# Two gated attention and expert layers on one core: the first norms' statistics on other engines, value gates as columns of the value product, slot tables in 16-bit pairs

## The chip, the cores and the metric

The kernel runs on one core of one Trainium2 chip. The metric is device time in microseconds for one launch. The text speaks of five engines: TensorE (PE; PEld is its weight load), VectorE (DVE), ScalarE (ACT), GpSimd (POOL) and SyncE (SP, which here only issues DMAs). L1691 is line 1691 of the kernel.

## The reference

`x` holds 16 sequences of 128 tokens of 256 values: T = 2048 tokens. Four residual steps follow each other:

```python
x = x + tanh(g_xattn[0]) * layernorm(x) * scan(0.9, ctx * ctx)        # along the sequence
x = x + tanh(g_ffn[0])   * moe0(layernorm(x))    # 8 experts, top 2 by softmax, capacity 640, gelu(a) * g, F = 512
x = x + tanh(g_xattn[1]) * attention(layernorm(x), ctx, ctx)          # causal and padding mask, bias in q, k, v
x = x + tanh(g_ffn[1])   * moe1(layernorm(x))    # 8 experts, top 2 by logits, silu, F = 1024
```

The experts work on rows that their router has chosen. In moe0 a row beyond an expert's capacity is dropped, so the place of each row in its expert's list has to be known: it is the count of earlier rows with the same choice.

## The kernel before

Tokens lie in 16 tiles of 128 rows (one tile is a sequence), taken in four quads q of four tiles (NQ = 4, QB = 4). `xs` holds x, `cx` the context, each 128x4096 in fp32. Every engine has its own program, written out by hand; what orders them is semaphores, and on each engine the order of the calls. `link` makes VectorE wait for its own instruction.

**Prologue** (from the start to the first expert product at L1691). Per quad: VectorE takes the statistics of the norm of x (`norm_stats(0, q)`, L991 and L994: four BATCH_NORM_STATS2 and four aggregates), ScalarE makes rstd of them (`root`, L656 and L658), VectorE the product mean x rstd (`coefs`, L1002), ScalarE the normalised rows (`normalise`, L665). GpSimd squares the context quad (L497); TensorE multiplies it by the decay triangle (`retention`, L1556: two fp32 products of 512 columns, four records); VectorE multiplies rows and retained context (`retained`, L1038) and adds them to xs (`added`, L1044). TensorE turns the new rows (`rows`, L1516), ScalarE copies them out of PSUM (`rows_out`, L692), and TensorE makes the router's logits (`rows_router`, L1522, 16 records of 8 columns). The logits need no normalised rows: the gate matrix has its column means taken off it beforehand (`router_sums`, `sums_out`, L1063), and 1/std scales a row's logits only where probabilities are wanted. VectorE takes the two best (`choose`, L1009 and L1012). The statistics of the second norm, on the rows after the addition, are again bn_stats on VectorE (`norm_stats(1, q)`), and ScalarE writes the rows normalised by them (`normalise1`), which SP stores to `xn_rows[0]` in DRAM.

Between these, TensorE also makes products which only the attention stage uses: the turned context (`context`), its values (`values`, L1522, 16 records of 256 columns), the product Wq^T Wk with its bias terms (`weights`), and the value gates: Wv^T times the second router's matrix (`value_weights`), then context times that (`value_gates`, 16 records of 8 columns), which VectorE adds a bias to (L1138). `busy(n)` is n products of constants with no use for their result.

**Tables** (layer 0). `one_hots` (L1087 to L1092), a product with a triangle (`ranks`, L1659 to L1663), `pick` (L1102 to L1110): each row's place in its expert's list, split into the number of a 128-slot block and the slot in it. `maps` writes three one-hot arrays in 16-bit floats: `oha` (L1123; which of NA = 46 blocks, for the 32 groups of rows), `by_slot` (L1127; the same times the slot's number, from `slot_wide`), and `ohb` in four parts (L1131; which of 128 slots; 128x1024 each). `invert` (L1671, 32 products) turns them into a list of row numbers by slot. `turned_slots` (L1115, L1116) makes `row_x`, and GpSimd gathers the rows by indirect DMA, 128 a time (`gather0`, L519), once `xn_rows[0]` is complete. `gates0` (L1167 to L1179) makes the gates out of the probabilities. TensorE turns the gathered rows (`xt0`, L1703), ScalarE and VectorE split them into a high and a low part (L742, L1208), and the experts begin (`hid0`, `out0`, L1691). Each expert takes its weights from `raw`, split in the same way (`win0`, `wout0`; L733 and L1197, L738 and L1203).

**Transition and attention** (240 to 321 us). After expert 7: `context(2)`, `context(3)`, `value_gates(2)`, `value_gates(3)`, `values(2)`, `values(3)`, 16 fillers, and then per quad `rows_turned`, `queries`, `router(1, t)`, `scores`, `mixed`, `attended`. VectorE meanwhile adds the experts' results (`joined(0)`: L1265 and the statistics), then runs `value_gates(3)`, `values_joined(2)` (L1279), `coefs(2, 0)`. GpSimd does a part of the additions (`share`). Then the tables of layer 1 follow in the same form as in layer 0, and 20 pairs of row tiles through layer 1's experts.

The core of the VectorE order before:

```python
norm0(0); slot_wide copy; coefs(0, 0); retained(0); added(0)
norm0(1); coefs(0, 1); norm_stats(1, 0); norm0(2); retained(1); coefs(1, 0); added(1); coefs(0, 2)
wg minus its means; norm_stats(1, 1); norm0(3); retained(2); added(2); coefs(1, 1); coefs(0, 3)
cb copy; norm_stats(1, 2); retained(3); added(3); norm_stats(1, 3)
choose(0); coefs(1, 2); choose(1); coefs(1, 3); choose(2); choose(3); one_hots(0)
```

## Time and profile before

| | |
|---|---|
| median of 3 runs | 570.4 us (569.59 to 573.92) |
| the profiled execution | 573.94 us, of which its span is 572.0 us |
| granted TensorE clock, mean over the span | 0.967 of full speed |
| busy in the span: PE, PEld, DVE, ACT, POOL | 531.3, 492.7, 350.6, 321.8, 254.4 us |
| prologue, to the first expert product | 76.1 us |
| layer 0 experts | 76.1 to 239.7 us |
| transition and attention, tables of layer 1 | 239.7 to 332.5 us |
| layer 1 experts and output | 332.5 to 572.0 us |

The times of the trace count from the start of the span. "Busy" of PE counts a product of 8 columns like one of 512 as busy for its own time. PEclk is the share of full clock granted in a stretch: 1.00 is 2.4 GHz and 0.50 is 1.2 GHz. The chain of waits is followed back from the last instruction; what is in it sets the end, as the rest lies beside it.

### The profile page before, as it was taken

What the parts mean: (1) busy time and instruction counts of PE and PEld (TensorE: products, weight loads), DVE (VectorE), ACT (ScalarE), POOL (GpSimd) and SP (SyncE); (2) the same over time, 40 slices, a digit from 0 to 9 for tenths busy, and PEclk for the clock granted to TensorE, in tenths of its full rate; (3) what the DMA queues carried; (4) which work ended last, traced back from release to release, by engine and by line L of the source; (5) the groups of instructions that cost most, each with busy time, mean ns of one, the idle gap of its engine ahead of it and who ended that gap; (6) DMA issues with size and microseconds to landing.
All of it is one profiled execution on the core that took longest, in us unless ns stands there. A gap on an engine that the chain in (4) does not pass through costs nothing.

```text
span 572.0 us, 11981 instructions
## 1 busy us (share of the span) xinstructions
PE 531.3 (93%) x3775; PEld 492.7 (86%) x3776; DVE 350.6 (61%) x834; ACT 321.8 (56%) x670; POOL 254.4 (44%) x284
## 2 busy tenths in 40 slices
PE   2899889999999999998996989999999999999993
PEld 1789789999999999986775879999999999999993
DVE  2888845765655675466687865565736574654742
ACT  3573345665656675425577646565746574654742
POOL 2400366664355542314000263555566456654554
PEclk9997699999999999979999899999999999999997
DMA  7944253445345353362023343654563545262233
GB/s 251 383 173 149 74 159 100 159 151 171 92 151 170 113 170 110 120 202 94 1 92 130 85 136 98 176 136 110 110 128 74 165 110 121 45 184 55 39 50 48
DMA packets 52453, 72.74 MB, mean 127 GB/s; under 512 B 7200, under 2 KB 43936, under 8 KB 52416
## 3 DMA queue, kind: packets, MB, share of 16 engines
q1 hardware_dynamic: 40752, 50.34, 27.3%
q0 software_dynamic: 11664, 21.94, 17.6%
q8 instruction: 19, 0.31, 0.2%
q14 instruction: 18, 0.15, 0.1%
HBM read 51.54 MB, written 20.73 MB: 126 GB/s over the span
## 4 chain that ended last, share of the span: by engine, by line
PE 80%; DVE 9%; DMA 3%; ACT 3%; issue 2%; POOL 1%; DVEq 0%; SPq 0%; POOLq 0%; ACTq 0%
PE PA L1691 27%; PE PD L1691 9%; PE PC L1691 8%; PE PC L1905 6%; PE PD L1905 6%; PE PC L1907 3%; PE PD L1907 3%; PE PB L1522 3%; PE PC L1522 2%; PE PD L1522 2%; PE PB L1703 2%; DMA xg<-xn_rows,row_x 2%; PE PB L1880 2%; DVE stats L991 1%; DMA cx<-ctx 1%
## 5 line engine op out<-in xcount | busy, mean ns | idle before, releaser
L1691 PE MATMUL PA<-xhi,w_parts 128*128 128x256 f32 (+1 forms) x880 | 182.8, 289 | 4.2 <-issue 2.1
L1691 PEld LDWEIGHTS PA<-xhi,w_parts 128*128 128x128 f32 x880 | 144.9, 190 | 8.1 <-issue 4.5
L1691 PE MATMUL PA<-xlo,w_parts 128*128 128x256 f32 (+1 forms) x440 | 125.9, 286 | 0.0
L1251 DVE TENSOR_TENSOR hlo<-cT_all,hhi 128x512 fp32r<-128x512 f32 x78 | 54.1, 693 | 96.7 <-ACT hhi L938 96.6
L936 ACT ACTIVATE cT_all<-PA 128x512 f32<-128x512 f32 x78 | 46.7, 599 | 91.2 <-PE PA L1691 90.4
L610 POOL DMA_INDIRECT out<-ys,row_o x38 | 65.0, 1712 | 71.2 <-DVE ys L1462 56.7
L1691 PEld LDWEIGHTS PA<-xlo,w_parts 128*128 128x128 f32 x440 | 83.7, 190 | 0.0
L519 POOL DMA_INDIRECT xg<-xn_rows,row_x x45 | 46.2, 1028 | 66.9 <-DVEq L1117 39.9
L528 POOL DMA_INDIRECT y_rows<-ys,row_y x40 | 41.8, 1045 | 55.5 <-ACT ys L763 53.3
L1905 PE MATMUL PC<-w_parts,hhi 128*128 128x512 f32 x160 | 58.4, 399 | 0.0
L586 POOL DMA_INDIRECT xg<-xn_rows,row_x x44 | 47.7, 1085 | 23.6 <-POOL slot_gate L604 8.7
L1691 PE MATMUL PC<-xhi,w_parts 128*128 128x256 f32 (+1 forms) x256 | 55.1, 293 | 0.0
L1905 PE MATMUL PD<-w_parts,hhi 128*128 128x512 f32 x144 | 52.5, 399 | 0.0
L1691 PE MATMUL PD<-w_parts,hhi 128*128 128x256 f32 x280 | 51.7, 285 | 0.4 <-DVE w_parts L1203 0.4
L938 ACT ACTIVATE hhi<-cT_all 128x512 fp32r<-128x512 f32 x78 | 49.3, 632 | 2.5
L1251 DVE TENSOR_TENSOR w_parts<-raw,w_parts 128x512 fp32r<-128x512 f32 x64 | 40.6, 686 | 10.4 <-ACT w_parts L805 10.2
L1907 PE MATMUL PC<-w_parts,hlo 128*128 128x256 f32 x160 | 45.0, 281 | 0.0
L1691 PEld LDWEIGHTS PD<-w_parts,hhi 128*128 128x128 f32 x280 | 43.6, 191 | 0.6 <-issue 0.6
L1691 PEld LDWEIGHTS PC<-xhi,w_parts 128*128 128x128 f32 x256 | 43.0, 190 | 0.0
L1907 PE MATMUL PD<-w_parts,hlo 128*128 128x256 f32 x144 | 40.5, 282 | 0.0
L1691 PE MATMUL PD<-w_parts,hlo 128*128 128x256 f32 x140 | 39.6, 283 | 0.0
L1691 PE MATMUL PC<-xlo,w_parts 128*128 128x256 f32 (+1 forms) x128 | 37.5, 293 | 0.0
(267 smaller groups left out, 1069.2 us busy)
## 6 DMA issues: line engine op xcount, KB each, us to landing
raw<-w SPq DMA_DIRECT2D x16, 1024.0 KB, 5.4
raw<-L_ffn_W_in SPq DMA_DIRECT2D x8, 1024.0 KB, 5.3
raw<-L_ffn_W_out SPq DMA_DIRECT2D x8, 512.0 KB, 4.0
y_rows<-ys SPq DMA_DIRECT2D x8, 512.0 KB, 6.8
xn_rows<-xn SPq DMA_DIRECT2D x8, 512.0 KB, 3.6
xs<-x SPq DMA_DIRECT2D x4, 512.0 KB, 7.4
cx<-ctx SPq DMA_DIRECT2D x4, 512.0 KB, 7.9
ys<-y_rows SPq DMA_DIRECT2D x4, 512.0 KB, 4.6
```

Source lines behind the costliest of these rows:

```text
L519: pool.indirect_dma_start(xg[:, s, :], None, xn_rows[0].ap(), bass.IndirectOffsetOnAxis(ap=row_x[:, e % E * CT + t:e % E * CT + t + 1], ax ...
L528: pool.indirect_dma_start(y_rows.ap(), bass.IndirectOffsetOnAxis(ap=row_y[:, e * CT + t:e * CT + t + 1], axis=0), ys[:, s, :], None).then_ ...
L586: pool.indirect_dma_start(xg1[j % SLOTS1], None, xn_rows[1].ap(), bass.IndirectOffsetOnAxis(ap=row_x[:, j:j + 1], axis=0)).then_inc(g1_in[ ...
L610: pool.indirect_dma_start(out, bass.IndirectOffsetOnAxis(ap=row_o[:, j:j + 1], axis=0), ys[:, j % SLOTS1, :], None, compute_op=ALU.add).th ...
L936: act.activation(group1(h1, g), PA[:, g % 2, :], ACT.Silu).then_inc(silu_done, 1)
L938: act.activation(group1(hhi, g), group1(h1, g), ACT.Copy).then_inc(h1_hi, 1)
L1251: return dve.tensor_tensor(dst, src, hi.bitcast(F32), ALU.subtract)
L1522: mm = pe.matmul(dst, a, b, start=(k == 0), stop=(k == len(lhs) - 1))
L1691: mm = pe.matmul(dst, a[k], b[k], start=(first and k == 0 and a is lhs_hi and b is rhs_hi), stop=(last and k == n - 1 and a is lhs_lo))
L1703: mm = pe.transpose(bank0(pair)[:, t - tiles_of(pair)[0], k, :], xg[:, s, k * P:(k + 1) * P], ident)
L1905: pe.matmul(y1_at(par, t), hhi[:, a:a + P], w_parts[:, :, at], start=(g == 0 and n == 0), stop=False)
L1907: mm = pe.matmul(y1_at(par, t)[:, 0:D], hlo[:, a:a + P], whi[:, at], start=False, stop=(g == GROUPS - 1 and n == 1))
```

## The change

It does seven things.

1. The second norm's mean comes from the router's product: the first gate matrix gets a ninth column of -1/256, so `lg[..., 8]` is minus the mean. ScalarE takes the variance with four Square activations and their accumulator per quad (`squares1`), and the root (`root1`). The four `norm_stats(1, q)` and `coefs(1, q)` leave VectorE. The rows are normalised by GpSimd (quads 0, 1, 3; four tensor_scalar each, after a product of its own) and by VectorE (quad 2, behind `one_hots(0)`), and by ScalarE no more.
2. SP's queue is reordered: x0, gates, ctx0, tables, x1, ctx1, the two routers' matrices, x2, ctx2, x3, ctx3, and then the attention's weights and biases. `load(0, 0, True)` goes ahead of the stores of `xn_rows`.
3. VectorE squares context quad 0, GpSimd the other three. The copies of `cb` and of the number tables are GpSimd's; `slot_wide` is gone.
4. TensorE's `context(0)`, `values(0)`, `weights`, `value_weights` go behind the four routers, on both sides of `ranks(0)`; the separate `value_gates` products are gone.
5. The value gates are eight more columns of the value product (`wide_values`: 264 columns); ScalarE copies values and gates out in four instructions a quad.
6. `oha`, `by_slot`, `ohb` are laid out in pairs of groups, and all operands of the three comparisons and products are 16-bit floats; in both layers.
7. In the transition the order on VectorE is `wide_gates(2)`, `values_joined(2)`, `joined(0)`, `wide_gates(3)`, `coefs(2, 0)`; the last values go out by ScalarE and get their bias from GpSimd; layer 1's first weight parts are made between the last five outputs of expert 7; 32 fillers for 16.

```diff
+        rhs_a = xflat[:, 0:MAP_BLOCKS * NA * NG // 2].bitcast(F16)\
+            .rearrange("p (m a g) -> p m a g", m=PAIRS_OF_GROUPS, g=PART)
+        by_slot, oha = (rhs_a[:, :, n * NA:(n + 1) * NA, :] for n in range(MAP_BLOCKS))
...
                 if q == 0:
-                    sp.dma_start(cf[:, :], cf_d).then_inc(cf_in, 16)
+                    sp.dma_start(gts[:, 0:2], g_xattn.partition_broadcast(P)).then_inc(g_in, 16)
+                    sp.dma_start(gts[:, 2:4], g_ffn.partition_broadcast(P)).then_inc(g_in, 16)
                 sp.dma_start(cx[:, q * QB:(q + 1) * QB, :],
                              ctxt[q * QB:(q + 1) * QB].rearrange("b p d -> p b d")).then_inc(ctx_in[q], 16)
                 if q == 0:
-                    sp.dma_start(gts[:, 0:2], g_xattn.partition_broadcast(P)).then_inc(g_in, 16)
-                    sp.dma_start(gts[:, 2:4], g_ffn.partition_broadcast(P)).then_inc(g_in, 16)
...
+                    sp.dma_start(cf[:, :], cf_d).then_inc(cf_in, 16)
+                if q == 1:
                     for n, w in enumerate((wg0, wg1T)):
-                        sp.dma_start(wg[:, n, :, 0:E], w.rearrange("(c p) e -> p c e", p=P)).then_inc(small_in, 16)
+                        sp.dma_start(wg[:, n, :, 0:E], w.rearrange("(c p) e -> p c e", p=P)).then_inc(wg_in, 16)
+            for n, w in enumerate((wq, wk, wvT)):
+                sp.dma_start(wqkv[:, n, :, :] if n < 2 else wvx[:, :, 0:D],
+                         w.rearrange("(c p) d -> p c d", p=P)).then_inc(small_in, 16)
+            for n, b in enumerate((bq, bk, bvc)):
+                sp.dma_start(bqk[:, n, :], b).then_inc(small_in, 16)
+            sp.dma_start(bvb[:, :], bv.partition_broadcast(P)).then_inc(small_in, 16)
...
+            sp.wait_ge(ret_done, NQ)
+            load(0, 0, True)
             for q in range(NQ):
-                if q == NQ - 1:
-                    sp.wait_ge(ret_done, NQ)
-                    load(0, 0, True)
-                sp.wait_ge(xn_ready, XN[1, q])
+                if q == 2:
+                    sp.wait_ge(xn1_vector, 1)
+                else:
+                    sp.wait_ge(xn1_pool, min(q, 2) + 1)
...
+            pool.wait_ge(cf_in, 16)
+            pool.tensor_copy(number_table[:, :, :], c("iota").unsqueeze(2).broadcast_to([P, P, PART]))
+            pool.tensor_copy(slot16[:, :], c("slot")).then_inc(table_ready, 1)
+            for t in range(1, NQ):
                 pool.wait_ge(ctx_in[t], 16)
                 if t >= 2:
                     pool.wait_ge(ret_done, t - 1)
                 pool.tensor_tensor(cx2[:, t % 2], cx[:, t * QB:(t + 1) * QB, :], cx[:, t * QB:(t + 1) * QB, :],
                                    ALU.mult).then_inc(sq_ready, 1)
...
+            pool.tensor_copy(cb[:, :], cf[:, CF["before"][0]:CF["ones"][1]]).then_inc(cb_ready, 1)
+            pool.wait_ge(small_in, 16 * 7)
+            pool.tensor_tensor(bqbk[:, :], bqk[:, 0, :], bqk[:, 1, :], ALU.mult).then_inc(wide_ready, 1)
+            for k in range(DC):
+                pool.tensor_tensor(bv_wide[:, k, :], c("ones"), bqk[:, 2, k:k + 1].broadcast_to([P, P]),
+                                   ALU.mult).then_inc(wide_ready, 1)
+            for q in range(NQ):
+                m = place(1, q)
+                pool.wait_ge(sd_ready, ROOT[1, q])
+                pool.tensor_tensor(nmr[:, m, :], lg[:, q * QB:(q + 1) * QB, E], rstd[:, m, :], ALU.mult)\
+                    .then_inc(coef1_ready, 1)
+                if q != 2:
+                    pool.wait_ge(coef1_ready, q + 1)
+                    pool.wait_ge(xn_out0[q % 2], 16 * (q // 2))
+                    for b in range(QB):
+                        ins = pool.tensor_scalar(xn[:, q % 2, b, :], xs[:, q * QB + b, :], rstd[:, m, b:b + 1],
+                                                 nmr[:, m, b:b + 1], ALU.mult, ALU.add)
+                    ins.then_inc(xn1_pool, 1)
...
+            share(1)
+            for n in range(3 * QB, 4 * QB):
+                value_bias(n)
+            for q in range(2, NQ):
...
+            def squares1(q):
+                act.wait_ge(lg_used, q + 1)
+                for b in range(QB):
+                    ins = act.activation(junk1[:, b, :], xs[:, q * QB + b, :], ACT.Square,
+                                         bias=lg[:, q * QB + b, E:E + 1], accum_out=mv[:, place(1, q), b, 1:2])
+                ins.then_inc(square1_ready, 1)
+            def root1(q):
+                act.wait_ge(square1_ready, q + 1)
+                root(1, q, scale=1.0 / D)
...
             root(0, 0)
             normalise(0, 0, xn0[0])
-            context_out(0)
             root(0, 1)
             normalise(0, 1, xn0[1])
+            sums_out()
+            rows_out(0)
+            root(0, 2)
+            normalise(0, 2, xn0[0])
+            squares1(0)
+            root(0, 3)
+            rows_out(1)
+            normalise(0, 3, xn0[1])
+            root1(0)
+            rows_out(2)
+            squares1(1)
+            root1(1)
+            rows_out(3)
+            squares1(2)
+            root1(2)
+            squares1(3)
+            root1(3)
+            weights_out()
+            value_weights_out()
+            context_out(0)
             values_out(0)
...
+            context_out(1)
             act.wait_ge(e_arg, 1)
...
+            for t in range(CT):
+                evac0(1, E - 1, [t])
+                if t < PIECES:
+                    split1(win_in[1], 16, win_hi[1], piece_in, (t,))
+            context_out(2)
+            context_out(3)
...
+            def normalised1(q):
+                m = place(1, q)
+                dve.wait_ge(coef1_ready, q + 1)
+                dve.wait_ge(xn_out0[q % 2], 16 * (q // 2))
+                for b in range(QB):
+                    ins = dve.tensor_scalar(xn[:, q % 2, b, :], xs[:, q * QB + b, :], rstd[:, m, b:b + 1],
+                                            nmr[:, m, b:b + 1], ALU.mult, ALU.add)
+                ins.then_inc(xn1_vector, 1)
             norm0(0)
-            dve.wait_ge(cf_in, 16)
-            link(dve.tensor_copy(slot_wide[:, :, :], c("slot").unsqueeze(2).broadcast_to([P, NG, NA])))
+            dve.wait_ge(ctx_in[0], 16)
+            dve.tensor_tensor(cx2[:, 0], cx[:, 0:QB, :], cx[:, 0:QB, :], ALU.mult).then_inc(square0_ready, 1)
             coefs(0, 0)
+            norm0(1)
+            coefs(0, 1)
             dve.wait_ge(tanh_ready, 1)
             retained(0)
             added(0)
-            norm0(1)
-            coefs(0, 1)
-            norm_stats(1, 0)
-            norm0(2)
-            retained(1)
-            coefs(1, 0)
-            added(1)
-            coefs(0, 2)
             dve.wait_ge(evac_done, EV1["s", 0])
+            dve.memset(wg[:, 0, :, E:E + 1], -1.0 / D)
             link(dve.tensor_tensor(wg[:, :, :, 0:E], wg[:, :, :, 0:E],
                                    wg_mean[:, :, :].unsqueeze(2).broadcast_to([P, 2, DC, E]), ALU.add))
             dve.sem_inc(wg_ready, 1)
-            norm_stats(1, 1)
+            norm0(2)
+            retained(1)
+            coefs(0, 2)
+            added(1)
+            copied(0)
             norm0(3)
             retained(2)
+            coefs(0, 3)
             added(2)
-            coefs(1, 1)
-            coefs(0, 3)
-            link(dve.tensor_copy(cb[:, :], cf[:, CF["before"][0]:CF["ones"][1]]))
-            dve.sem_inc(cb_ready, 1)
-            norm_stats(1, 2)
+            chosen(0)
+            copied(1)
             retained(3)
             added(3)
-            norm_stats(1, 3)
-            choose(0)
-            coefs(1, 2)
-            choose(1)
-            coefs(1, 3)
-            choose(2)
-            choose(3)
+            chosen(1)
+            copied(2)
+            chosen(2)
+            copied(3)
+            chosen(3)
...
+            def maps(layer):
+                def over_pairs(x, m, n):
+                    return x[:, m.start * PART:m.stop * PART].rearrange("p (m g) -> p m g", g=PART).unsqueeze(2)\
+                        .broadcast_to([P, m.stop - m.start, n, PART])
+                every = slice(0, PAIRS_OF_GROUPS)
+                dve.tensor_tensor(oha, over_pairs(high16, every, NA), number_table[:, 0:NA, :].unsqueeze(1)
+                                  .broadcast_to([P, PAIRS_OF_GROUPS, NA, PART]), ALU.is_equal).then_inc(oha_ready, 1)
+                dve.tensor_tensor(by_slot, oha, over_pairs(slot16, every, NA), ALU.mult).then_inc(slot_ready, 1)
                 for n in range(MAP_PARTS):
+                    m = slice(n * PAIRS_OF_GROUPS // MAP_PARTS, (n + 1) * PAIRS_OF_GROUPS // MAP_PARTS)
+                    dve.tensor_tensor(ohb[:, m, :, :], over_pairs(low16, m, P), number_table[:, :, :].unsqueeze(1)
+                                      .broadcast_to([P, m.stop - m.start, P, PART]), ALU.is_equal)\
                         .then_inc(map_ready, 1)
...
             one_hots(0)
+            normalised1(2)
...
             masks()
             split1(0, win_hi[1], win_lo[1], piece_in)
-            value_gates(2)
+            wide_gates(2)
...
+            values_joined(2)
             joined(0)
-            value_gates(3)
-            values_joined(2)
+            wide_gates(3)
             coefs(2, 0)
             for t in range(NQ - 1):
                 joined(t + 1)
                 if t >= 2:
                     attended(t - 2)
                 coefs(2, t + 1)
-                if t == 0:
-                    values_joined(3)
...
+            def wide_values(q):
+                pe.wait_ge(evac_done, max(EV1["cT", q], EV1["v", 0]) if q == 1 else EV1["cT", q])
                 cT = context_at(q)
                 for b in range(QB):
-                    mm = product(values_at(q)[:, b // 2, (b % 2) * D:(b % 2 + 1) * D],
-                                 [cT[:, k, b * P:(b + 1) * P] for k in range(DC)],
-                                 [wqkv[:, 2, k, :] for k in range(DC)])
+                    mm = product(value_banks(q)[b // 2][:, b % 2, 0:D + E],
+                                 [cT[:, k, b * P:(b + 1) * P] for k in range(DC)], [wvx[:, k, :] for k in range(DC)])
                 mm.then_inc(evac_ready, 1)
...
+            busy(2, early_fill)
             retention(0)
-            context(0)
-            busy(4)
-            values(0)
+            router_sums()
             retention(1)
             rows(0)
-            router_sums()
-            weights(0)
             retention(2)
-            weights(1)
+            rows_router(0)
+            retention(3)
             rows(1)
-            retention(3)
-            rows_router(0)
-            busy(5, PA)
+            pe.wait_ge(ret_used, 3)
+            busy(4, early_fill)
+            rows_router(1)
             rows(2)
-            rows_router(1)
-            busy(11, PA)
+            busy(4, early_fill)
+            rows_router(2)
             rows(3)
-            rows_router(2)
+            busy(4, early_fill)
             rows_router(3)
-            value_weights()
-            busy(6, PB)
...
+            weights(0)
             pe.wait_ge(cb_ready, 1)
             ranks(0)
-            value_gates(0)
+            weights(1)
+            value_weights()
+            context(0)
+            wide_values(0)
+            invert(0)
             context(1)
-            busy(9)
-            invert(0)
-            value_gates(1)
-            values(1)
-            pe.wait_ge(evac_done, EV1["v", 1])
+            wide_values(1)
...
+            pe.wait_ge(evac_done, EV1["cT", 1])
+            xt0(0, 0, 0, 0, filler=1)
             xt0(0, 0, 0, 1, filler=1)
+            pe.wait_ge(evac_done, EV1["v", 1])
             pe.wait_ge(target0_ready, 1)
...
             context(3)
-            value_gates(2)
-            value_gates(3)
-            values(2)
-            values(3)
-            for n in range(16):
-                pe.matmul(PA[:, 0, 0:P], ident, decay, start=True, stop=True)
+            pe.wait_ge(y0_evac, 2 + E * CT)
+            wide_values(2)
+            wide_values(3)
+            pe.wait_ge(values2_ready, 1)
+            pe.wait_ge(vg_ready, 3)
+            for n in range(32):
+                pe.matmul(PC[:, 0, 0:P], ident, decay, start=True, stop=True)
```

## Rows read from the trace of the kernel before

**Rows 1.** The page's chain that ended last: shares of the span by engine

```profile
PE 80%; DVE 9%; DMA 3%; ACT 3%; issue 2%; POOL 1%; DVEq 0%; SPq 0%; POOLq 0%; ACTq 0%
```

**Rows 2.** Chain of waits, 8 to 77 us: start us, length us, what

```profile
1.77 6.49 DMA cx<-ctx
...
62.89 3.35 PE PA L1522 x16
...
66.25 5.56 PE PC L1522 x16
...
71.83 1.03 ACT vv L687
...
76.12 1.00 PE PA L1691 x5
```

**Rows 3.** Timeline of VectorE, 0 to 95 us: start us, length us, then what

```profile
4.26 1.40 DVE L991 BATCH_NORM_STATS2 stats<-xs 128x6 f32<-128x256 f32 x4 [4.15 <-DMA xs<-x]
...
14.27 1.28 DVE L1038 SCALAR_TENSOR_TENSOR xg<-xg,tg,PA 128x1024 f32<-128x1024 f32 x1 [3.00 <-PE PA L1556]
...
19.56 1.88 DVE L1002 SCALAR_TENSOR_TENSOR nmr<-mv,rstd 128x4 f32<-128x4 f32 x1 [0.66 <-ACT rstd L658]
...
50.40 0.19 DVE L1087 CAST eidx<-topi 128x32 f32<-128x32 uint32 x1
...
54.85 1.69 DVE L1123 TENSOR_TENSOR xg<-sm,cf 128x1472 f16<-128x1472 f32 x1
...
56.57 0.93 DVE L1127 TENSOR_TENSOR xg<-xg,slot_wide 128x1472 f16<-128x1472 f16 x1
...
57.42 4.62 DVE L1131 TENSOR_TENSOR ys<-smi,cf 128x1024 f16<-128x1024 int32 x4
...
68.03 0.29 DVE L1167 TENSOR_REDUCE rr<-lg 128x16 f32<-128x128 f32 x1 [0.24 <-DVE vg L1138]
...
70.50 0.26 DVE L1179 TENSOR_TENSOR gates<-sm,rr 128x16 f32<-128x16 f32 x2
```

**Rows 4.** Timeline of ScalarE, 0 to 95 us

```profile
11.37 2.07 ACT L665 ACTIVATE xg<-xs,nmr,rstd 128x256 f32<-128x256 f32 x4 [0.37 <-DVEq L1003]
...
58.44 1.99 ACT L733 ACTIVATE w_parts<-raw 128x1024 fp32r<-128x1024 f32 x2
```

**Rows 5.** Timeline of TensorE, 0 to 80 us

```profile
10.37 3.75 PE L1556 MATMUL PA<-raw,cf 128*128 128x512 f32 x4 [10.37 <-POOL raw L497]
...
29.67 1.11 PE L1522 MATMUL PD<-wqkv 128*128 128x256 f32 x4
...
30.62 1.04 PE L1516 MATMUL PB<-cf,xs 128*128 128x128 f32 x8
...
33.21 1.85 PE L1522 MATMUL PD<-wg,xT 128*128 128x8 f32 x16
```

**Rows 6.** Timeline of GpSimd, 0 to 95 us

```profile
19.52 1.89 POOL L497 TENSOR_TENSOR raw<-cx 128x1024 f32<-128x1024 f32 x1 [0.80 <-DMA cx<-ctx]
...
64.27 1.14 POOL L519 DMA_INDIRECT xg<-xn_rows,row_x  x1 [39.93 <-DVEq L1117]
...
67.70 0.95 POOL L519 DMA_INDIRECT xg<-xn_rows,row_x  x1 [0.30 <-issue]
...
82.14 0.76 POOL L510 TENSOR_TENSOR vv<-vv,bvb 128x256 f32<-128x256 f32 x1
```

**Rows 7.** Busy time of each engine, PEclk and DMA in one stretch

```profile
66.00:68.00 2.00, 2.00 (x7) 1.64 (x7) 1.79 (x3) 0.00 (x0) 1.70 (x2) 0.50 0.23 66
```

**Rows 8.** Chain of waits, 225 to 262 us

```profile
252.51 3.45 PE PC L1522 x16
```

**Rows 9.** Timeline of VectorE, 236 to 296 us

```profile
256.03 1.23 DVE L1279 TENSOR_TENSOR vv<-PB,bvb 128x1024 f32<-128x1024 f32 x1
```

**Rows 10.** Chain of waits, 300 to 344 us

```profile
314.12 2.09 ACT xT L868 x8
...
320.93 4.71 DMA xn_rows<-xn
```

268 lines of the change are left out of this document (115 added, 153 removed).

## The prediction

> **What bounds the kernel now.** I read the page's chain first: TensorE carries 80% of what sets the end [rows 1], nearly all in expert products that the change doesn't touch. So the change can only move three stretches in which TensorE is not simply full of expert work: the prologue, the transition to attention, and the tables of layer 1. The chain of waits of the prologue [rows 2] is mixed: the context's DMA, then VectorE and TensorE in turns, and at the end, after the table product, two products for the attention stage (value gates 3.35 us, values 5.56 us), a copy of 1.03 us, and then the first expert product at 76.12. The reader is to see two things. First, 9 us of TensorE work that nobody needs before 250 us stands between the finished tables and the first expert. Second, the tables start only at 50.40 [rows 3], since VectorE's program before them is long.
>
> **VectorE up to the tables.** Gone are four second-norm statistics (1.40 of bn_stats [rows 3], 0.38 of aggregates and two waits on itself, 1.97 each, 7.9 in all), four coefficient products (0.31 with the wait, 1.2), slot_wide (0.93) and the cb copy (0.3): 10.3 us. Added is the square of context quad 0, by the 1.28 of an operation of that size [rows 3], in time that was idle. New times, step by step. The context quad 0 landed at 8.26 behind x0 and the tables [rows 2]; now it lands near 6.3 and the tables, without which TensorE and ScalarE don't start, near 8.3, as the bytes up to there are the same. ScalarE's root is ready at 9.1, the normalised rows (2.07 [rows 4]) at 11.5, the first retention (3.75 [rows 5]) at 12.6. From VectorE's first statistics at 4.26 up to retained(1) there are 11.0 us of its work: three norm statistics 5.9, the square 1.25, two coefficients 0.6, one retained and one added 2.8, the gate matrix 0.4. Its waits: tables and root 1.55, x1's landing 0.65, root 0.7, and three collisions with GpSimd. These are the row at 19.56 [rows 3]: a product of 4 columns took 1.88 us, elsewhere 0.16, and it ended with GpSimd's square that began at 19.52 and took 1.89 [rows 6]. GpSimd's squares now fall near 11.6, 14.3 and 17.5, where VectorE has coefs(0,1), added(0) and the gate matrix product, all with both inputs in SBUF. I take 0.8, 1.05 and 1.0. Sum: 4.26 + 11.0 + 5.75 = 21.0 for retained(1).
>
> From there to the tables VectorE has 16.6 us: three retained and three added 8.4, one norm statistics 2.0, two coefficients 0.6, four copies of logits 1.4, four choices 4.2. It waits 1.9 for the last router, since the turned rows (1.04), ScalarE's copy (1.03), the fillers and 16 router records (1.85) follow each other [rows 2, 5]. The tables start at 21.0 + 16.6 + 1.9 = 39.5 against 50.4.
>
> The Trainium skill, in "SBUF — State Buffer" under "Who interferes with whom", says that a VectorE instruction with two SBUF inputs and a GpSimd one that reads SBUF exclude each other for a whole instruction. The row at 19.56 agrees. It speaks against this change, which gives GpSimd twelve normalisations in this very stretch. By the rule these 2.9 us of collisions and the ones below stand; without it everything would come about 2.5 us earlier.
>
> **The tables.** The first comparison (fp32 number table, 1.69) and the product of the same 1472 columns with all operands in 16 bits (0.93) show what width does [rows 3]. All three forms are 16-bit now: 1.69 to 0.93, 0.93 unchanged, 4.62 to about 2.6 for four parts. No row has an inner run of two elements, so the bounds are no gain and the 0.93 rate; I take the rate, as its row is the nearest in size and type. Ahead of them stand the normalisation of quad 2 on VectorE (four of 128x256, between 1.0, the rate of a one-input copy, and 1.9, that of two inputs) and pick, 2.2 as before. Tables done: 39.5 + 1.7 + 1.2 + 2.2 + 4.5 = 49.1, and up to 51.5 if GpSimd's last quad comes in between (four instructions of about 0.6).
>
> On TensorE the last router ends at 38.0. Then weights(0) 2.1 (1.11 [rows 5] and as much for the bias columns), ranks at 41.6, weights(1) 2.1, value weights 1.4 (12 records by 1.85/16), turned context 1.04, ScalarE's copy with its hand-overs 1.2, wide values 3.6 (3.45 [rows 8] for 264 instead of 256 columns): 50.9. So TensorE and the tables meet at about 51, and whether the 16-bit rate holds costs up to 2 us and no more. The 32 inversion products need 1.7: the row list is ready at 52.6, before at 62.89.
>
> **From the row list to the first expert.** Two paths. By the gathers: the first followed the list's end by 1.4 [rows 2, 6], the third starts 3.4 behind it, lands about 3 later, and turning and splitting takes 1.5: 62.2. By the values: ScalarE copies out values(0) with the gates in 1.4 (to 52.4), splits the first weights in 1.99 [rows 4] (54.4), copies the context (55.4); wide_values(1) ends at 59.1, its copy at 60.5. Behind that on VectorE is value_gates(1), 0.3, and behind this stand gates0, from 68.03 to 70.76 [rows 3], 2.7 us which before ran while TensorE still made values(1). Now this cover is gone. Then the low parts, 1.2: first expert product at 65.0. TensorE is idle there for about 4 us, so I add 1.0 for a lower clock in the first expert: 66.0. The prologue gives 76.1 - 66.0 = 10.1 us.
>
> GpSimd's normalisations: a two-input operation of this size takes 0.76 [rows 6], one column 0.2; these have one input, I take 0.6. Quads 0 and 1 run near 31 and 36, quad 3 near 42 to 47, its store lands near 51. The gather waits for it at 54.0, so 3 us hide it. SP's new order costs nothing: the attention's weights are wanted at 38, and loads and zero fills are out by then.
>
> **Transition.** VectorE does values_joined(2), 1.23 [rows 9] and a wait, while it still waits for the experts' results, and values_joined(3) goes to ScalarE and GpSimd. coefs(2,0) could move up by 1.4, but rstd is there only 1.0 earlier, and GpSimd's four bias additions (0.76 each) now collide with coefs and the next additions. I take 0.5. TensorE does the same value work, without 32 records of 8 columns (4.9 us), but with 16 fillers more (3.7): it fits if the clock holds, and if it fell, it would lose up to 1.5. Bounds -1.5 and 1.0.
>
> **Tables of layer 1.** 2.8 us of VectorE go, 0.2 come. The chain there runs beside them: squares 2.09, normalise, then the rows' store from 320.93 for 4.71 us [rows 10], which ends at 325.6, 0.5 behind the row list. I take 0; the bounds are 0 and 0.3, because the gathers have to wait for the store anyway.
>
> **Sum.** 10.1 + 0.5 = 10.6. The profiled span goes from 572.0 to 561.4, and with the 1.9 around it the execution from 573.9 to 563.3. That execution lay 3.5 over the median of the runs, so the median goes from 570.4 to 559.8.
>
> **Rivals.**
>
> A: less waiting. The squares miss VectorE's two-input steps, and the clock holds all through. Then 2.5 to 3.5 more: 556.5. For it: the collisions depend on tenths of a microsecond. Against: VectorE has such steps in half of its time.
>
> B: TensorE at half clock behind the routers. In 66 to 68 it was granted 0.50 [rows 7], and 16 value records took 5.56 [rows 2] where 3.45 [rows 8] is the price at full clock; ahead of that were products of 8 columns and gaps. The change still has router products of 9 columns with only 4 fillers between, where before it was 5 and 11. The work on the path behind the tables (2.1, 1.4, 1.0, 3.6, 3.6: 11.7) would take 1.6 times as long: 7 us back, 566.8. Against it: the wide products now stand together and fill the array, and the slow stretch before began only behind 28 us of such a mix.
>
> C, the other side: GpSimd's normalisations decide. Twelve stand in series with nothing else able to do them, from 31 on, and the gather waits for the store of the last. At 0.6 they are hidden. The path is old if the list's last row is stored at 65.5 (76.1 less 8.2 from gather to product and 2.4 for the row's turn at the queue), so from (65.5 - 3.5 - 31)/12 = 2.6 us each the kernel is slower. At 4 us, with scalar pointers handled slowly and every one blocked by VectorE, they end at 79, and the kernel takes 570.4 + 17 = 587. For it: no row here has that operation on GpSimd. Against: 0.76 for two inputs.
>
> D: the change does not do what it says, as the moved products only move the bound: the first expert waits for gates0 and the values, and both prove a few microseconds longer than worked out. Gain 5: 565.5.
>
> **Chances.** Forecast 0.50, A 0.22, B 0.15, C 0.03, D 0.10. The range for 8 in 10 takes A in and most of B and D: 554 to 567. A measurement of this kernel tells about 1% (5.7 us) from no change; below 564.7 lie the forecast, A and some of B and D: 0.84. Within 1% are most of B and D: 0.13. Slower is C: 0.03.
>
> **What would show it.** Right: VectorE's eidx at 38 to 41; first L1691 product at 64 to 67, its last releaser on VectorE behind gates0; the three table forms at 0.93, 0.93 and 0.65 each; coefs of 4 columns that take over 1 us beside GpSimd. Layer 1's store of rows still ends its chain. Wrong: a granted clock of 0.5 between 40 and 60 (B); gathers that are released by the store of `xn_rows` (C); a first expert before 63 (A); expert stages of another length than before, which nothing here explains.

## The result, and the profile after

The changed kernel takes 576.33 us, the median of 20 runs (572.08 to 584.94), and the kernel before 571.0 us beside it (20 runs, 569.14 to 576.41). Six of the 20 runs of the changed kernel fell into a slower state of the machine (581.39 to 584.94 us), and the ratio leaves them out. It is 1.0058, with a 95% interval of 1.0036 to 1.008: slower by half a per cent, where 559.8 us was forecast. The profiled execution lasts 575.3 us with a span of 573.4, against 573.9 and 572.0 before.

The chain of waits of the prologue after the change (start us, length us, what), which answers to [rows 2]:

```profile
12.86 1.22 DVE nmr L1047
...
15.76 2.53 DVE xs L1090
...
18.53 1.74 DVE wg L1114
...
30.93 3.21 PE PD L1586 x16
...
47.27 3.41 PE PC L1586 x12
50.68 2.36 PE PA L1586 x12
53.04 1.81 PE PB L1580 x8
...
55.96 3.89 PE PA L1586 x8
59.84 2.25 PE PC L1586 x8
...
63.36 1.89 ACT w_parts L770 x2
...
77.43 2.81 PE PA L1742 x10
```

VectorE in the same prologue, which answers to [rows 3]:

```profile
44.55 0.19 DVE L1138 CAST eidx<-topi 128x32 f32<-128x32 uint32 x1
...
50.07 0.92 DVE L1179 TENSOR_TENSOR xg<-high,number_table 128x1472 f16<-128x1472 f16 x1
51.03 0.93 DVE L1182 TENSOR_TENSOR xg<-xg,slot 128x1472 f16<-128x1472 f16 x1
51.87 2.49 DVE L1185 TENSOR_TENSOR ys<-low,number_table 128x1024 f16<-128x1024 f16 x4
...
63.48 0.21 DVE L1166 CAST row_y<-PD 128x46 int32<-128x46 f32 x1 [8.16 <-PE PD L1720]
...
75.77 0.26 DVE L1246 TENSOR_TENSOR gates<-sm,rr 128x16 f32<-128x16 f32 x2
```

VectorE's program was shortened as intended: its statistics are gone, the three table forms take 0.92, 0.93 and 2.49 us, and eidx comes 5.9 us earlier than at [rows 3] (10.9 were forecast). But the row list is read at 63.48, and before it was read at 63.49. In between VectorE waits 8.16 us for TensorE. The gain of the first half of the prologue is gone by the list, and the first expert product comes at 77.43 instead of 76.12.

The busy times in four stretches of 8 us show why (after the stretch and its length: TensorE's products, its weight loads, VectorE, ScalarE and GpSimd, then PEclk, the DMA share and GB/s). Before:

```profile
28.00:36.00 8.00, 8.00 (x52) 6.41 (x51) 6.96 (x21) 5.82 (x19) 0.00 (x0) 1.00 0.96 336
36.00:44.00 8.00, 7.42 (x67) 7.17 (x65) 6.73 (x22) 6.15 (x12) 0.00 (x0) 1.00 0.13 47
44.00:52.00 8.00, 8.00 (x49) 7.90 (x48) 6.47 (x57) 2.87 (x8) 0.00 (x0) 0.64 0.45 140
52.00:60.00 8.00, 6.20 (x58) 5.82 (x57) 7.06 (x12) 4.45 (x7) 0.00 (x0) 0.93 0.27 107
```

After:

```profile
28.00:36.00 8.00, 6.65 (x34) 6.65 (x35) 5.12 (x17) 3.98 (x12) 2.37 (x5) 0.62 1.08 391
36.00:44.00 8.00, 7.78 (x65) 7.59 (x64) 4.17 (x33) 7.43 (x25) 2.56 (x6) 0.93 0.40 144
44.00:52.00 8.00, 8.00 (x32) 7.03 (x32) 7.28 (x24) 2.97 (x16) 2.70 (x5) 0.50 0.44 153
52.00:60.00 8.00, 6.89 (x22) 5.63 (x23) 3.22 (x8) 1.28 (x3) 0.00 (x0) 0.50 0.01 3
```

A busy TensorE says little here: in 44 to 52 it is busy all the time, at 0.50 of its clock, its level of 1.2 GHz. The record counts don't compare like with like, as the queues differ, but the same product does: four records of 256 columns with the attention's weights take 2.05 us there and 1.11 at [rows 5]. TensorE in the changed kernel, at the two falls of its clock:

```profile
29.35 1.58 PE L1609 MATMUL PA<-cf 128*128 128x128 f32 x8 [2.09 <-DVEq L1086]
...
41.05 1.95 PE L1586 MATMUL PD<-wg,cT_all 128*128 128x9 f32 x16 [0.22 <-ACT cT_all L722]
...
43.30 1.60 PE L1586 MATMUL PC<-bqk,wqkv 128*128 128x1 f32 x8
44.76 2.05 PE L1586 MATMUL PC<-wqkv 128*128 128x256 f32 x4
```

Ahead of the fall near 30 it had waited 2.1 us. Ahead of the one near 44 came 16 records of router products, nine columns each, and then products of one column.

Of the milestones, each from the profile of its kernel (us from the span's start):

| kernel | eidx | row list | first expert product | span | eidx to list | list to product |
|---|---|---|---|---|---|---|
| before | 50.40 | 63.49 | 76.12 | 572.0 | 13.09 | 12.63 |
| changed | 44.55 | 63.48 | 77.43 | 573.4 | 18.93 | 13.95 |
| forecast | 39.5 | 52.6 | 65.0 | 561.4 | 13.1 | 12.4 |
| b_nofill | 52.00 | 64.88 | 78.61 | 575.8 | 12.88 | 13.73 |
| b_tables | 48.57 | 58.46 | 69.83 | 567.6 | 9.89 | 11.37 |
| a_head | 42.87 | 61.82 | 74.23 | 572.5 | 18.95 | 12.41 |
| a_fill | 42.44 | 56.20 | 68.61 | 567.5 | 13.76 | 12.41 |
| a_gates | 43.22 | 62.17 | 71.95 | 567.4 | 18.95 | 9.78 |
| a_ctx | 46.69 | 65.64 | 77.30 | 574.4 | 18.95 | 11.66 |
| a_all | 41.65 | 54.26 | 64.38 | 561.6 | 12.61 | 10.12 |
| a_all_again | 41.73 | 54.33 | 64.46 | 561.3 | 12.60 | 10.13 |
| a_wide | 42.46 | 56.19 | 66.31 | 562.3 | 13.73 | 10.12 |
| a_squares | 40.97 | 53.58 | 63.69 | 562.2 | 12.61 | 10.11 |
| a_vbias | 42.89 | 55.50 | 65.71 | 564.5 | 12.61 | 10.21 |
| a_best | 40.48 | 53.08 | 63.20 | 558.1 | 12.60 | 10.12 |
| p_scalar | 42.07 | 54.67 | 64.79 | 559.7 | 12.60 | 10.12 |
| p_tensor | 42.00 | 54.60 | 64.72 | 563.0 | 12.60 | 10.12 |
| p_gpsimd | 41.64 | 54.23 | 64.35 | 560.1 | 12.59 | 10.12 |

The forecast put the first expert product itself at 65.0; its 66.0 holds 1.0 for slower products behind it. The miss of the span is 12.0 us (573.4 less 561.4). At the first expert product it is 12.4 already, in three parts: 5.05 up to eidx, 5.8 from there to the list (18.93 for 13.1), 1.5 behind the list (13.95 for 12.4).

Not every difference in this table is an effect. Up to eidx the changed kernel, a_gates and a_ctx run the same program, and their profiles have it at 44.55, 43.22 and 46.69. The way from eidx to the list is steadier: 18.93 to 18.95 in the four versions without added products behind the last router, and 12.59 to 13.76 in the ten with them.

### The profile page after: what moved, and what is told of

Same layout as the page of the kernel before. It is cut to its first block, busy times and chain, and to the rows that moved or that the text cites. A ratio compares the mean times of both kernels' runs of the same rounds, so it can differ in the third digit from the quotient of the medians.

```text
span 573.4 us, 11834 instructions
## 1 busy us (share of the span) xinstructions
PE 527.2 (92%) x3697; PEld 487.2 (85%) x3698; DVE 343.5 (60%) x805; ACT 323.7 (56%) x695; POOL 261.8 (46%) x306
## 4 chain that ended last, share of the span: by engine, by line
PE 75%; DVE 9%; issue 7%; DMA 3%; ACT 3%; POOL 1%; SPq 0%; DVEq 0%; ACTq 0%; POOLq 0%
PE PA L1742 28%; PE PC L1742 8%; PE PD L1742 8%; PE PC L1958 6%; PE PD L1958 6%; PE PC L1960 3%; PE PD L1960 3%; PE PD L1586 2%; PE PC L1586 2%; DVE xs L1333 2%; PE PB L1933 2%; DVE stats L1036 1%; PE PC L1609 1%; PE PB L1754 1%; PE PB L1586 1%
## 5 line engine op out<-in xcount | busy, mean ns | idle before, releaser
L637 POOL DMA_INDIRECT out<-ys,row_o x38 | 64.2, 1689 | 70.5 <-DVE ys L1526 60.4
L543 POOL DMA_INDIRECT xg<-xn_rows,row_x x45 | 46.3, 1029 | 45.8 <-PE PB L1754 16.4
```

The lines of the kernel that those rows point to most:

```text
L543: pool.indirect_dma_start(xg[:, s, :], None, xn_rows[0].ap(), bass.IndirectOffsetOnAxis(ap=row_x[:, e % E * CT + t:e % E * CT + t + 1], ax ...
L637: pool.indirect_dma_start(out, bass.IndirectOffsetOnAxis(ap=row_o[:, j:j + 1], axis=0), ys[:, j % SLOTS1, :], None, compute_op=ALU.add).th ...
```

## Experiments

All ratios are to the kernel before, run beside them. Two kernels of this list are compared by their ratios.

**TensorE's clock, in the changed kernel.** a_fill adds products that nobody reads:

```diff
             retention(1)
+            busy(9, PB[:, 0, 0:P])
             rows(0)
...
             rows(1)
-            pe.wait_ge(ret_used, 3)
-            busy(4, early_fill)
+            busy(12, PD[:, 1, 0:P])
             rows_router(1)
             rows(2)
-            busy(4, early_fill)
+            pe.wait_ge(ret_used, 3)
+            busy(6, early_fill)
             rows_router(2)
             rows(3)
-            busy(4, early_fill)
+            busy(6, early_fill)
             rows_router(3)
+            busy(6, early_fill)
...
             context(0)
+            busy(4, PA[:, 1, 0:P])
             wide_values(0)
...
             context(1)
+            busy(8, late_fill)
             wide_values(1)
...
             xt0(0, 0, 0, 1, filler=1)
+            busy(16, late_fill)
```

> The changed kernel with more fillers on TensorE: 9 before rows(0), 12 for 4 before the second router, 6 for 4 before the third and fourth, 6 behind the fourth, 4 and 8 in the waits for the two context copies, 16 behind the first gathered rows. Nothing else changes. Theory 1, the lost gain is TensorE's clock (0.50 in 30 to 36, 44 to 61 and 68 to 71 us, and again in the first expert, from 77 to 81): the granted clock stays at 1.00 through most of the prologue, the list of rows is ready at 54 to 57 us instead of 63.5, the first expert product comes at 68 to 71 instead of 77.4 and the kernel takes 565 to 569 us. Theory 2, the order of the steps and waits costs it (gates0 behind value_gates(1), the weight splits ahead of the context copy, GpSimd's collisions): the fillers only add work, first product at 77 or later, 575 to 579 us.

Measured: 567.39 us, ratio 0.986 (0.9811 to 0.9909). No work was taken away, 55 products were added, and by the ratios the kernel became about 2% faster than the changed one (the profiled spans differ by less, 5.9 us). The same stretches:

```profile
28.00:36.00 8.00, 8.00 (x75) 8.00 (x73) 6.29 (x18) 6.27 (x17) 2.37 (x5) 1.00 1.08 394
36.00:44.00 8.00, 8.00 (x72) 7.95 (x72) 4.86 (x42) 7.31 (x27) 2.56 (x6) 1.00 0.45 165
44.00:52.00 8.00, 8.00 (x51) 7.61 (x50) 7.57 (x17) 2.26 (x10) 2.70 (x5) 0.79 0.39 133
52.00:60.00 8.00, 7.92 (x74) 7.12 (x73) 4.27 (x13) 5.14 (x10) 2.71 (x2) 1.00 0.05 16
```

and two of the products on the path, from TensorE's timeline of a_fill:

```profile
31.06 1.85 PE L1586 MATMUL PD<-wg,cT_all 128*128 128x9 f32 x16
...
50.93 2.09 PE L1586 MATMUL PA<-wvx,cT_all 128*128 128x264 f32 x8
```

By the chain of waits and the timeline of the changed kernel they took 3.21 and 3.89 there. The row list comes 7.3 us earlier, the first expert product 8.8. The clock was not held all through: it was at 0.50 from 24 to 27 and, behind the 12 records of 8 columns of `value_weights`, from 48 to 51. In a_all, which has the same fillers there, it stayed at 1.00 from 44 to 56, and so it did in the seven other profiles with 12.59 to 12.61 from eidx to the list. The run also moves one wait (`ret_used`) behind the second router. That isn't tested by itself, but the second router starts at 31.06, no earlier than in the changed kernel (30.93).

**Which half of it.** a_head has these fillers only ahead of the last router (the 9, 12, 6 and 6, and the moved wait), none behind it.

> The changed kernel with the added fillers only where they stand ahead of the last router (9 before the first rows are turned, 12 and 6 and 6 before the routers after it, the wait for the retained parts one step later); nothing is added behind the last router. With fillers in both places the tables' first step was at 42.44 and the list of rows at 56.20 (changed kernel: 44.55, 63.48). Theory (each half of the queue pays by itself for its gaps): the first step at 42.2 to 43.2, the list of rows at 60 to 62.5, first expert product at 73.5 to 76.5 and a time 1 to 3 us under the changed kernel. Rival (it is enough that the routers run at full clock, the clock then stays for the products behind them): the list at 56 to 58 and the whole gain of 8 us.

Measured: 574.19 us, ratio 1.001 (0.9983 to 1.0037). The list comes 1.7 us earlier than in the changed kernel, all of it up to eidx; behind the last router the clock falls as before, and the way from eidx to the list stays at 18.95. So the products behind the routers are the larger part: of a_fill's 7.3 us at the list, 5.6 lie between a_head and a_fill. The 1.7 ahead of eidx would be within what single profiles vary, but the six profiles with these fillers have eidx at 41.65 to 42.89 and the three without at 43.22 to 46.69. The first expert product follows the list by 12.41 in both a_head and a_fill, for 13.95: in the changed kernel the last value products ran partly at 0.50 (5.4 us for 3.7).

**The same in the kernel before.** b_nofill takes its prologue fillers out. The wait that stood inside the first `busy` on PA is kept:

```diff
-            busy(4)
             values(0)
...
-            busy(5, PA)
+            pe.wait_ge(ret_used, NQ - 1)
...
-            busy(11, PA)
...
-            busy(6, PB)
...
             context(1)
-            busy(9)
```

> The kernel before without the prologue's filler products (4, 5, 11, 6 and 9 of 128 columns); what they compute is not read. Theory (the engine's clock falls when its queue of routers and table products has gaps, and that is what the changed kernel lost): the granted clock shows 0.50 earlier and for longer than in before (there from about 60 to 70 us), above all between 28 and 60; the routers' product of 16 by 9 columns goes from 2.2 to over 3 us; the list of rows, at 63.49 in before, moves to 64.5 to 68, the first expert product from 76.12 to 78 to 82, and the time is 1 to 5 us above before. Rival (before is held by VectorE in the prologue, so the clock matters only where TensorE sets the end): the one-hot tables start where they did (50.4) and the list of rows is within 1 us, the time within 1.5 us of before. Rival 2 (fillers only stand in the way): faster by 1 us or more.

Measured: 578.43 us, ratio 1.0078 (1.0044 to 1.0113), the clock from its windows:

```profile
36.00:44.00 8.00, 5.54 (x35) 5.44 (x35) 6.81 (x22) 5.47 (x12) 0.00 (x0) 0.62 0.15 54
44.00:52.00 8.00, 8.00 (x39) 8.00 (x39) 5.04 (x55) 3.36 (x7) 0.00 (x0) 0.50 0.46 141
52.00:60.00 8.00, 6.68 (x32) 5.99 (x32) 6.96 (x14) 1.11 (x3) 0.00 (x0) 0.50 0.17 69
```

The clock is at 0.50 from 37.9 to 72.0 here; in the kernel before it was at 0.50 from 46.3 to 53.1 and from 59.9 to 70.1. So the 35 fillers held its clock over a part of the prologue and were worth 0.8%, some 4.5 us by the ratio (3.8 in the profiled span). It shows up to eidx (1.6) and behind the list (1.1), not between.

**The tables alone.** b_tables is the kernel before with only the paired 16-bit tables; VectorE makes the number table, since GpSimd's part of the change is left out.

```diff
-            link(dve.tensor_copy(slot_wide[:, :, :], c("slot").unsqueeze(2).broadcast_to([P, NG, NA])))
+            link(dve.tensor_copy(number_table[:, :, :], c("iota").unsqueeze(2).broadcast_to([P, P, PART])))
+            link(dve.tensor_copy(slot16[:, :], c("slot")))
...
-            maps(0, sm[:, 3, :])
+            maps(0)
```

> The kernel before with only the 16-bit tables in pairs (both layers); the number tables are made by VectorE where slot_wide was. The three table forms take 0.93, 0.93 and 2.5 us instead of 1.69, 0.93 and 4.62, so in layer 0 the list of rows should be ready 2.8 us earlier and the first expert product too, as TensorE's work behind the tables moves up with it: 567.5 to 568.5 us. In layer 1 nothing, because the store of the rows ends the chain there. If TensorE's clock takes part of it back, 569 to 571.

Measured: 570.67 us, ratio 0.9964 (0.994 to 0.9988). The forms are 0.93, 0.93 and 2.49 as in the changed kernel, the list comes at 58.46 and the first expert product at 69.83. By itself this part is a gain, of 0.1 to 0.6%. Of the 5.0 us at the list only 3.2 are the tables'. The other 1.8 lie ahead of eidx: the product of 4 columns that took 1.88 beside GpSimd's square at [rows 3] took 0.47 in this profile, as the square missed most of it.

**The gates' place.** a_gates moves one call on VectorE:

```diff
+            gates0()
             value_gates(1)
             dve.sem_inc(hid0_used, 2)
-            gates0()
```

> The changed kernel with gates0() moved ahead of value_gates(1) on VectorE; nothing else changes. In the changed kernel gates0 takes from 73.4 to 76.2 us in front of the low parts which the first expert waits for, while VectorE was idle from 67.8 to 73.0. Theory 2: the first expert product comes 2.7 us earlier, at 74.7, TensorE has a wait of 1.7 instead of 4.4 us before it, and so the first expert runs at full clock (1.8 us more): 4 to 4.5 us less in all. Theory 1 alone: 2.7 us of it at most, and with the clock moved about, anything from 0 to 4.

Measured: 573.89 us, ratio 1.0013 (0.9981 to 1.0044). VectorE's timeline of a_gates:

```profile
69.17 0.26 DVE L1246 TENSOR_TENSOR gates<-sm,rr 128x16 f32<-128x16 f32 x2
70.03 0.19 DVE L1192 TENSOR_TENSOR vg<-vg,vg_bias 128x32 f32<-128x32 f32 x1 [0.59 <-ACT vg L717]
```

The twelve small steps are now done while the second values are still being copied. From the list to the first expert product it is 9.78 us instead of 13.95. Beside a_head and a_fill with their 12.41, some 2.6 of this is the gates' place; the other 1.5 is the clock in the last value products, which took 3.7 us here and 5.4 in the changed kernel. The eidx that comes 1.3 earlier is no effect of this edit.

**ScalarE's order.** a_ctx puts the first values and the second context copy ahead of the splits of the first weights:

```diff
-            values_out(0)
...
+            values_out(0)
+            context_out(1)
             for k in range(DC):
                 win0(0, k)
-            context_out(1)
```

> The changed kernel with ScalarE's queue alone reordered: the first values and the second context copy go ahead of the two splits of the first expert's weights (63.22 for 2.02 us), no fillers and the gates where they were. Theory (the copy at 65.11 stands 2 us behind the splits, and the second values, the gates and the first product wait for it in a row): the copy at 63.2 to 63.8, second values done at 69.5 to 70, first expert product at 75 to 76 against 77.43, the time 1 to 2.5 us under the changed kernel (about 574 to 575 beside 576.3). Rival (the splits then come late and VectorE's low parts, which stand ahead of both parts of the value gates, hold the first product in their place): first product at 77 to 78 and no change.

Measured: 573.05 us, ratio 1.0033 (0.9998 to 1.0067). The prologue ahead was 2.2 us later in this profile (list at 65.64), so the times of day that were expected missed; from the list on the order holds: the copy comes 0.9 us behind it instead of 1.6, and the first expert product 11.66 behind it instead of 13.95 (12.41 where the clock is full). So the order is worth 0.7 us. The ratio alone doesn't tell it from the changed kernel.

**Together.** a_all has the fillers (2 instead of the last 16), the gates and ScalarE's order.

> The changed kernel with the fillers of a_fill (2 for 16 behind the gathered rows), gates0() ahead of value_gates(1), and on ScalarE both copies (values(0), context(1)) ahead of the first weight splits. If both theories hold in part, their gains add: first expert product at 63 to 66 us, 560 to 564 us for the kernel. If the clock is all, it is at the time of a_fill within 1 us less; if the order is all, at that of a_gates less 2.

Measured: 563.4 us, ratio 0.9809 (0.9755 to 0.9862). Run once more (a_all_again):

> The kernel with fillers, gates first and early context copy once more, as the measure for the two beside it: 563 to 564 us, first gelu at 69 to 70.5, some 5.3 us behind the first expert product.

Measured: 564.29 us, ratio 0.9872 (0.982 to 0.9924), first gelu 5.08 behind the first product. The two ratios show how much the pairing with other runs leaves open: about 0.6%.

**The collisions.** a_squares, on top of a_all:

```diff
             for t in range(1, NQ):
                 pool.wait_ge(ctx_in[t], 16)
+                if t == 1:
+                    pool.wait_ge(wg_ready, 1)
...
-            retention(1)
-            busy(9, PB[:, 0, 0:P])
+            busy(16, PB[:, 0, 0:P])
             rows(0)
+            retention(1)
+            rows_router(0)
             retention(2)
-            rows_router(0)
```

> The changed kernel with fillers, gates first and the early context copy (564 us, list of rows at 54.26), and in addition GpSimd's first square waits until VectorE has corrected the router's weights, so that its three squares of 1.89 us stand beside VectorE's statistics and its product with a PSUM operand; on TensorE the first rows are turned ahead of the second retention product. Theory (the small coefficients at 1.2 us, the addition at 2.5 and the weights' correction at 1.8 are each stretched by a GpSimd square beside them, by 1.05 + 1.3 + 1.6 us): these three take 0.16, 1.23 and about 0.2 to 0.5 us, other VectorE instructions that now meet a square are statistics and products from PSUM and keep 1.4 and 1.28; the tables' first step moves from 41.65 to 38 to 40, and the time falls by 1.5 to 3.5 us. Rival (the routers' chain on TensorE and ScalarE bounds this stretch by then): the three shorten, but the first step moves by less than 0.7 us and the time by less than 1.

Measured: 563.63 us, ratio 0.9837 (0.9791 to 0.9883). VectorE in a_squares:

```profile
12.92 0.16 DVE L1049 SCALAR_TENSOR_TENSOR nmr<-mv,rstd 128x4 f32<-128x4 f32 x1 [0.66 <-ACT rstd L687]
...
15.23 1.22 DVE L1092 TENSOR_TENSOR xs<-xs,xg 128x1024 f32<-128x1024 f32 x1
...
16.65 0.19 DVE L1116 TENSOR_TENSOR wg<-wg,wg_mean 128x32 f32<-128x32 f32 x1
16.98 1.41 DVE L1038 BATCH_NORM_STATS2 stats<-xs 128x6 f32<-128x256 f32 x4
...
21.10 1.28 DVE L1086 SCALAR_TENSOR_TENSOR ring<-ring,tg,PC 128x1024 f32<-128x1024 f32 x1 [2.30 <-PE PC L1623]
...
40.97 0.19 DVE L1140 CAST eidx<-topi 128x32 f32<-128x32 uint32 x1
```

The three steps shrink from 1.22, 2.53 and 1.74 to 0.16, 1.22 and 0.19, and the statistics and the product from PSUM, which now stand beside squares, keep 1.41 and 1.28. The cause of the stretching is shown. But eidx moves by 0.68 us only. Of the 3.9 us freed, 2.30 go at once to a wait for the second retention, which this run itself makes later, as its square now starts at 17.05 instead of 12.70. The other 1.6 reach ScalarE's copy of the second turned rows, which ends at 28.51 instead of 30.10. There 24 filler records on TensorE end only at 29.75, and the second router starts at 29.59 instead of 30.15: 1.0 is lost to the fillers. From that router to eidx it is 11.4 and 11.5 us. The time did not fall, as the rival said, but for these reasons as much as for the routers' chain.

**The last values' bias.** a_vbias, on top of a_all:

```diff
-            for n in range(3 * QB, 4 * QB):
-                value_bias(n)
...
                 coefs(2, t + 1)
+                if t == 0:
+                    dve.tensor_tensor(vv[:, 3 * QB:4 * QB, :], vv[:, 3 * QB:4 * QB, :],
+                                      bvb[:, :].unsqueeze(1).broadcast_to([P, QB, D]), ALU.add).then_inc(v_ready, 1)
```

> The same kernel of 564 us, and in addition the bias of the last four value tiles is added by VectorE behind the second part's coefficients of the attention stage, where it waits for TensorE anyway, not by GpSimd. Theory (GpSimd's 3.13 us of bias beside VectorE's sums of the second part, 2.53 and 2.34 against 1.28 and 1.99 before, and the coefficient at 0.73 against 0.15, is what this move cost): the sums return to 1.3 and 2.0, the second part's root comes 1.5 to 2 us earlier, the attention stage is 1 to 2 us shorter, and so is the time. Rival (the stage is bound by the rows' way through TensorE and ScalarE behind it, or VectorE's 1.23 us takes the place of what is saved): the stage and the time within 0.7 us, or longer.

Measured: 563.64 us, ratio 0.9811 (0.9774 to 0.9848). VectorE's timeline in a_all, with GpSimd's bias beside it:

```profile
247.10 2.65 DVE L1333 SCALAR_TENSOR_TENSOR xs<-xg,gates,xs 128x256 f32<-128x256 f32 x3
249.79 2.45 DVE L1333 SCALAR_TENSOR_TENSOR xs<-ring,gates,xs 128x256 f32<-128x256 f32 x3
```

and in a_vbias:

```profile
249.59 1.28 DVE L1331 SCALAR_TENSOR_TENSOR xs<-xg,gates,xs 128x256 f32<-128x256 f32 x3
250.91 1.28 DVE L1331 SCALAR_TENSOR_TENSOR xs<-ring,gates,xs 128x256 f32<-128x256 f32 x3
```

From the first turned rows of the attention stage to layer 1's ranks it is 51.66 us, in a_all 53.36, and before 51.64. The sums themselves are twice as fast. What the stage gains by it is less sure than the 1.7 of this pair: the nine profiles with GpSimd's bias have 51.84 to 54.58, the five without 51.66 to 53.15. In the time it can't be told from a_all.

**All of it.** a_best is a_all with a_squares and a_vbias.

> All that has helped so far together: fillers, gates first, early context copy, GpSimd's squares behind the correction of the weights, and the last values' bias on VectorE. Theory (the parts lie in different stages and add): tables' first step near 41, list of rows at 53.5, attention stage of 51.6 us instead of 53.4, time 561 to 563 us. Rival (what is gained ahead of the first expert and in the attention stage is spent in waits for rows and weights): within 0.5 us of the same kernel without the last two.

Measured: 562.13 us, ratio 0.9846 (0.9797 to 0.9895), profiled span 558.1, the shortest of all. The milestones are a_all's less 1.2 us, the stage is 51.67. a_all_again beside it has 0.9872: the step goes the right way by 0.3%, within what can be told. a_all, its repetition, a_squares, a_vbias, a_best and a_wide (below) all beat both kernels.

**What eats an early start.** In the versions that start the first expert earlier, ScalarE's first gelu lags. TensorE and ScalarE in a_all:

```profile
64.38 0.41 PE L1746 MATMUL PA<-xhi,w_parts 128*128 128x320 f32 x1 [1.96 <-DVE xlo L1275]
...
70.68 0.42 PE L1746 MATMUL PA<-xhi,w_parts 128*128 128x320 f32 x1 [2.08 <-DVE ring L1284]
```

```profile
62.86 0.67 ACT L774 ACTIVATE w_parts<-raw 128x512 fp32r<-128x512 f32 x1
69.66 0.44 ACT L787 ACTIVATE ring<-PA 128x320 f32<-128x320 f32 x1 [6.13 <-PE PC L1746]
```

The first group of twelve products is recorded as done at 66.41, and the gelu that reads it starts at 69.66, 5.28 behind the first product; before it was 2.06. Four runs asked whether instructions come late. a_wide has a_all's added fillers as products of 256 columns, half as many:

> The same kernel, with its added fillers of 128 columns in pairs as one of 256: the same filler work in 26 fewer products (and as many fewer weight loads). Where an earlier start of the first expert was followed by a first gelu 5.3 us behind the first product (2.06 in before), with nothing in the trace that ScalarE waited for, two reasons are open. Theory (TensorE's instructions were not there yet: one load of instructions falls into the same microsecond as the first product in every kernel of the changed family, at another place in before): with a shorter program the load lies elsewhere and the gelu comes 2 to 4 us behind the first product, the time 1 to 3 us lower. Rival (something of the start itself, such as weights or rows that land late, holds it): the gelu again 5 us or more behind, and the same time.

Measured: 563.26 us, ratio 0.9841 (0.9797 to 0.9885); the gelu came 4.32 behind the first product. That lies between the two expectations and settles nothing. Three more put 64 semaphore increments that nobody waits for ahead of one engine's wait for the tables, in a_best:

```diff
+            for n in range(64):
+                act.sem_inc(padding, 1)
             act.wait_ge(cf_in, 16)
```

> The fastest combination, with 64 semaphore increments that nobody waits for on ScalarE ahead of its wait for the tables, where it is idle: its program is the same, but lies 64 instructions further on. In every kernel of the changed family ScalarE's first gelu follows its last split of weights by 5.2 to 6.4 us, in before by 2.2, and in the combination it is 5.1 us behind the first expert product. Theory S (ScalarE's own instructions are late there): the gap changes by over 1 us with this pad and with no other. Theory T (TensorE's are late): unchanged here, 5 us behind the first product. Rival (neither: rows or a wait): unchanged with all three pads.

> The same with 64 increments on TensorE ahead of its wait for the tables. Theory T: the first gelu now follows the first expert product by 2 to 4 us, or by another amount than 5.1 by over 1 us, and the load of instructions that fell beside the first product lies elsewhere. Theory S and the rival: 5 us again.

> The same with 64 increments on GpSimd ahead of its wait for the tables. Theories S and T: 5 us again. A third, G (GpSimd, which issues the gathers there, is held by its instructions, and TensorE by the third pair of rows): another gap by over 1 us, here alone.

Measured in one execution each: 561.59, 564.83 and 561.93 us, with the kernel before at 573.55 beside them. The gelu came 5.21, 5.24 and 5.22 behind the first product, in a_best 5.07. But the one instruction load that falls beside the first product stays there in each (64.6, 64.6 and 64.2 us, for first products at 64.79, 64.72 and 64.35). So the padding did not move what it was to move, and late instructions are not excluded: in a_fill TensorE pauses twice inside the first products with nothing that it waits for (0.34 and 0.41, "issue"). What holds the gelu stays open. From the first product to the first transposes of the second expert it takes 18.2 to 18.4 us in eight of the nine profiles that show this wait (19.8 in a_all_again), and 16.06 before. Not all of these 2.2 us belong to the early start: the changed kernel, b_nofill and b_tables take 17.6 as well.

## Why the prediction was wrong

**What bounds the kernel.** Right in the main: the forecast was lost in the prologue. The expert stages changed their length too (sum below), which nothing here explains. What was read but not carried through is that the kernel before had fillers that held the clock in the very stretch that was to be rebuilt.

**VectorE up to the tables.** Forecast 39.5, measured 44.55. The collisions were seen in their three places, but mis-sized: 0.8, 1.05 and 1.0 forecast, 1.05, 1.3 and 1.55 measured (1.22, 2.53 and 1.74 less a_squares' 0.16, 1.22 and 0.19). retained(1) came at 22.46, not at 21.0. The other 3.6 us lie behind it, where the path leaves VectorE: the chain goes through turned rows, ScalarE's copy and the routers. Of these, some 2 are clock (a_fill brings eidx to 42.44), and some 1.4 remain at full clock: in a_fill the routers start at 31.06, 35.01 and 39.00, one every 4 us, as each set of rows goes through TensorE, ScalarE and TensorE again. The forecast gave that succession 1.9 us of waiting in all. The rule of the Trainium skill ("SBUF — State Buffer", "Who interferes with whom") agrees with these rows: VectorE's work on two SBUF inputs stretches beside GpSimd, its statistics and its product from PSUM do not. The saving of about 2.5 us that the prediction gave for a kernel without collisions did not come in a_squares (0.68). That run had costs of its own, a later square and fillers ahead of the second router, so the 2.5 is neither shown nor refuted.

**The tables.** Right: 0.92, 0.93 and 0.62 each, for 0.93, 0.93 and 0.65.

**TensorE behind the routers: the step that failed.** "The last router ends at 38.0 ... 50.9" priced every product at full clock, 12.9 us for weights, ranks, value weights, context and wide values. It took 19.1 (43.0 to 62.1). With the clock at 1.00, a_all needs 12.8 from its last router (40.1) to its wide values' end (52.9), with ten fillers that take 1.58 and 1.06 us, so the prices held and the clock did not. (1.5 of the 12.9 was a wait for the ranks that did not occur.) This was rival B, given 0.15 and 7 us; up to the wide values it cost 6.2, and 1.5 more behind the list. The kernel came out 9.5 us slower even than B's 566.8, as B stood for this stretch alone. What spoke against it, that "the wide products now stand together", did not help: they stood behind narrow ones, and the clock had fallen when they came. For it stood [rows 7], and that the changed queue had 4 fillers where 5 and 11 had been. It should have been the likelier case. The Trainium skill ("TensorE: Matmul & The Clock Gate", "HAM oscillation — how this bites in real kernels") tells of a clock that falls again and again where TensorE waits for data between short groups of products. The trace agrees in 28 to 36, behind a wait of 2.1 us; in 44 to 52 the clock is low with no such wait recorded. The runs with fillers show what the low clock cost there. What let it fall is not isolated: no run changed the width of the products alone.

**From the list to the first expert.** Forecast 12.4, measured 13.95, and 12.41 in the two profiles with the same order and a full clock there: the step was right, its 1.5 is the clock again. (The recorded terms add up to 64.7 and not 65.0, which changes nothing.) Both bounds were named: gates0 without its cover, some 2.6 us by a_gates, and the copy behind the splits, 0.7 by a_ctx. They were named as costs and left standing, though.

**GpSimd's normalisations.** Right: 0.54 to 0.63 each (2.17 and 2.50 for four), and nothing waited for their stores. Rival C is refuted.

**Transition.** Forecast 0.5 gained. From context quad 2's turn to the attention's first rows it is 19.70 us, before 19.80. But the collisions with the bias fall into the attention stage, which is 0.7 longer (52.37). a_vbias shows them in the sums (2.65 and 2.45 for 1.28 each); their cost for the stage is at most the 1.7 of that pair. The place was named, and their price, four times 0.76 beside VectorE's sums, was not carried to the end.

**Layer 1's tables.** Forecast 0, bounds 0 and 0.3. From the ranks to the first expert product of layer 1 it is 20.43 us instead of 21.36: 0.9, more than the bound.

**The first expert.** 1.0 was added for a lower clock; it took 1.5 more, at 0.50 in 78 to 80, and the whole of layer 0 took 1.8 more (165.4 against 163.6). But b_nofill and b_tables, whose experts are unchanged, have 165.6 and 166.1, so this can't be put down to the change.

**Sum.** Against the kernel before: first expert product +1.3, layer 0 +1.8, transition -0.1, attention +0.7, tables of layer 1 -0.9, layer 1 itself -1.4 (238.05 against 239.46; b_nofill has 238.5, so this too is within what profiles vary), together the span's +1.4. Against the forecast, 12.4 us are missing at the first expert product, and a_fill alone brings back 8.8 of them (2.1 up to eidx, 5.2 to the list, 1.5 behind it): rival B's mechanism. Collisions and the routers' succession are the rest. In the span a_fill brings back only 5.9 of the 12.0. Rival D was partly true (the first expert did wait for gates0, a_gates). Rival A's gain from missed collisions did not show in a_squares.

The median missed by more than the span, 16.5 us (576.33 less 559.8). The forecast took 3.5 off, because the profiled execution before lay that far above the median of three runs; the one of the changed kernel lies 1.0 below the median of its 20. These 4.5 us are no mechanism.

## What to carry to other kernels

Where a change re-orders a TensorE queue that has gaps or narrow products in it, price the work behind them at the clock that the trace shows behind such a mix, not at the price of the same product in a dense stage, and count the fillers of the old order as part of what is removed. The windows of PEclk show whether that happened; if it did, products that nobody reads can pay (here about 2% of the kernel). Before a milestone of one profile is called an effect, compare it with another profile of a program that is the same up to there: eidx varied by 3.5 us here. And work taken off the engine that bounds a stretch counts only down to the next chain, here four routers in a row through two engines: work out when that chain would end by itself.

## What was not expected of the hardware

The clock fell to 0.50 with TensorE recorded as busy for all of 44 to 52, behind products of nine columns and of one: its recorded busy time did not hold it up, while with wider fillers put between (in one of these runs 24 records of 128 columns, in 2.84 us) it stayed at 1.00 over 44 to 56 in eight of the ten profiles that have them. A comparison whose inner run is a pair of 16-bit numbers takes 0.93 us for 1472 columns, as much as the 16-bit product of that size. GpSimd's scaling and shift of 128x256 with columns as scalars takes 0.54 us (four in 2.17; up to 3.16 for four in a_all). And a wait of 5.1 to 5.3 us between a first product and its first reader, in nine profiles, with no releaser that fits: not explained.
